# Ternary layers in five groups instead of six, with seeded banks for the last two, another order of slots and state-space layer, and one branch

## What is computed

```
x = x + 0.5 * _L0_ffn_ref(_layernorm(x), W1, W2, W3)            # gated layer, hidden 2048
x = x + _L0_attn_ref(_layernorm(x), qkv, o_proj, gamma, beta)
x = x + 0.5 * _L0_ffn_ref(_layernorm(x), W1, W2, W3)
x = x + 0.5 * _L1_ffn_ref(_layernorm(x), gate_w, up_w, down_w, gate_s, up_s, down_s)
x = x + _L1_attn_ref(_layernorm(x), B, C, D)                    # state-space layer
x = x + 0.5 * _L1_ffn_ref(_layernorm(x), gate_w, up_w, down_w, gate_s, up_s, down_s)

def _L1_ffn_ref(x, ...):     # ternary layer, weights in {-1, 0, 1}, hidden 1408 = 11 blocks of 128
    g = einsum('th,ih->ti', x, gate_w) * gate_s
    u = einsum('th,ih->ti', x, up_w) * up_s
    return einsum('ti,hi->th', silu(g) * u, down_w) * down_s

def _L1_attn_ref(x, B, C, D):
    return einsum('bsn,dn->bsd', tanh(einsum('bsd,nd->bsn', x, B)), C) + D * x
```

## Time and profile before

| | |
|---|---|
| median of 3 runs | 1855.29 us (1854.92 to 1859.22) |
| the profiled execution | 1855.78 us, its span 1853.9 us |
| PE matmul busy, share of the span | 1743.8 us, 94% |
| VectorE (DVE) | 1199.1 us, 65% |
| ScalarE (ACT) | 824.2 us, 44% |
| GpSimd | 121.4 us, 7% |
| matmuls in the program | 7696 |

### The profile page before, as it was taken

How to read it: one execution, slowest core, us unless ns; L and a number is a source line. 1 busy time by engine, 2 the same in 40 slices (tenths; PEclk the granted TensorE clock), 3 DMA queues, 4 the chain that set the end, 5 groups by cost and what they waited for, 6 DMA issues and landing times.

```text
span 1853.9 us, 21200 instructions
## 1 busy us (share of the span) xinstructions
PE 1743.8 (94%) x7696; PEld 1407.2 (76%) x7696; DVE 1199.1 (65%) x1843; ACT 824.2 (44%) x1347; POOL 121.4 (7%) x184
## 2 busy tenths in 40 slices
PE   6899999999978999899999999999989987899998
PEld 5688887788867888688888888887767766677676
DVE  8777678577754555554447444467688676767866
ACT  4544544465654343333223343234554545454443
POOL 1000000000021210000000000000000505000000
PEclk9899999999999999999999999999999999899999
DMA  8675553799944000154444444444555541256464
GB/s 309 228 267 205 204 204 141 310 363 366 373 171 173 21 1 1 56 199 153 154 153 154 153 153 154 153 183 174 205 204 210 199 171 52 102 205 237 172 222 187
DMA packets 61403, 340.34 MB, mean 184 GB/s; under 512 B 6256, under 2 KB 14832, under 8 KB 43760
## 3 DMA queue, kind: packets, MB, share of 16 engines
q1 hardware_dynamic: 52848, 334.73, 47.9%
q10 hardware_dynamic: 8448, 4.20, 0.8%
HBM read 259.73 MB, written 79.17 MB: 183 GB/s over the span
## 4 chain that ended last, share of the span: by engine, by line
PE 45%; DVE 8%; ACT 2%; issue 2%; POOL 0%; DVEq 0%; ACTq 0%; POOLq 0%
PE psum L420 18%; PE psum L422 14%; PE psum L424 12%; DVE xc_lo L1561 1%; PE psum L614 1%; DVE sg L1631 1%; DVE stats L1487 1%; DVE y L1593 1%; DVE y L1596 1%; DVE x L1605 1%; ACT psum L1084 1%; ACT xc_hi L992 0%; DVE y L1599 0%; DVE sg L1624 0%; DVE x L1591 0%
## 5 line engine op out<-in xcount | busy, mean ns | idle before, releaser
L420 PE MATMUL psum<-xc_hi,w 128*128 128x512 f32 x1544 | 621.1, 402 | 48.9 <-ACT psum L1166 18.4
L422 PE MATMUL psum<-xc_lo,w 128*128 128x512 f32 x1544 | 609.1, 394 | 0.0
L420 PEld LDWEIGHTS psum<-xc_hi,w 128*128 128x128 f32 x1544 | 294.0, 190 | 142.6 <-ACT psum L1084 32.2
L420 PE MATMUL psum<-w,hid 128*128 128x512 f32 x896 | 357.5, 399 | 28.8 <-ACT xs L974 8.8
L424 PE MATMUL psum<-xc_hi,w 128*128 128x512 f32 x928 | 365.7, 394 | 0.0
L424 PE MATMUL psum<-w,hid 128*128 128x512 f32 x896 | 352.6, 394 | 0.0
L422 PEld LDWEIGHTS psum<-xc_lo,w 128*128 128x128 f32 x1544 | 294.5, 191 | 57.9
L1591 DVE TENSOR_TENSOR x<-psum,x 128x512 f32<-128x512 f32 x256 | 172.9, 687 | 151.9 <-PE psum L424 151.9
L420 PEld LDWEIGHTS psum<-w,hid 128*128 128x128 f32 x896 | 170.4, 190 | 80.5 <-ACT psum L1191 14.9
L1613 DVE TENSOR_TENSOR hid<-sg,hid 128x512 fp32r<-128x512 f32 x224 | 159.7, 713 | 99.6 <-ACT hid L1099 80.7
L422 PE MATMUL psum<-w,hid 128*128 128x512 f32 x544 | 213.5, 392 | 0.0
(11 more groups left out here) (151 smaller groups left out, 1992.5 us busy)
## 6 DMA issues: line engine op xcount, KB each, us to landing
w<-w_kept SPq DMA_DIRECT2D x93, 1792.0 KB, 7.3
w<-w_kept SPq DMA_DIRECT2D x94, 512.0 KB, 8.2
w_kept<-w SPq DMA_DIRECT2D x16, 1792.0 KB, 7.6
w_kept<-prep SPq DMA_DIRECT2D x12, 1792.0 KB, 7.5
w_kept<-w SPq DMA_DIRECT2D x16, 512.0 KB, 6.8
w_kept<-prep SPq DMA_DIRECT2D x12, 512.0 KB, 8.6
x<-in_w2a SPq DMA_DIRECT2D x8, 512.0 KB, 8.1
att_raw<-in_att_w SPq DMA_DIRECT2D x4, 1024.0 KB, 7.7
```

Source lines behind the costliest of these rows:

```text
L420: pe.matmul(out, a_hi, b_hi, start=start, stop=False, skip_group_check=onto)
L422: last = pe.matmul(out, a_hi, b_lo, start=False, stop=stop and zero == "a", skip_group_check=onto)
```

## The change

- Ternary groups are now `(0,1,2)`, `(3,4)`, `(5,6)`, `(7,8)`, `(9,10)`. The third block of the first group is kept in two parts of `xs` (`hid_more`).
- The down tiles of slots 1 and 2 are gone; the first group stands in slots 3 and 4 with 6 matmuls a tile.
- Of the group `(7,8)`, tiles 0 to 3 are made and added in slot 9 as before. Tiles 4 to 7 are made in a new step `fill`, after p4 of slot 10, in the banks in which the last group then goes on accumulating. The last group's eight tiles have a bank each: 0, 4, 1, 3, 2 for tiles 0 to 4 (`END_BANKS`) and the ring's for 5 to 7. All eight are seeded with `y`; tiles 5, 6, 7 already in slot 9.
- ACT does `seed_y` ahead of both `hid_high` of the block before, and in some slots (`open`: 1, 2, 10) one of these later still. DVE's work for the layer norm and the sums is spread by tables (`LATE`, `FINISH`, `STATS`, `SUMS`), also over the first slots of the next pass, which add the last tiles and take the last conversions. New waits (`ended_before`) keep the next pass off banks 0 to 4 until their tile is read.
- State-space layer: `STATE_ORDER`, the orders of DVE and ACT, and the place of one `chunk` of GpSimd.
- PE has one branch around passes 4 to 7 and the state-space layer, instead of two with the state-space layer between them.

```diff
-          "B": [(0,)] + [(2 * g - 1, 2 * g) for g in range(1, HB // P // 2 + 1)],
+          "B": [(0, 1, 2)] + [(2 * g + 1, 2 * g + 2) for g in range(1, HB // P // 2)],
...
+END_BANKS = (BX, BV, BY, BW, BZ)
+SEED_ORDER = (5, 6, 7, 0, 1, 4, 2, 3)
+FILL_ORDER = (5, 6, 7, 4)
...
+SUMS = {4: {7: (0,), 8: (1,), 9: (2, 3)}, 5: {}, 6: {8: (0, 1), 9: (2, 3)}, 7: {}}
...
-               ("down", 1, range(TT)), ("up", 2, ()), ("up", 3, ()), ("next", 0, range(TT)), ("down", 2, range(2)),
-               ("next", 1, range(TT)), ("down", 2, range(2, TT)), ("down", 3, range(TT))]
+               ("down", 1, range(TT)), ("up", 2, ()), ("next", 0, range(TT)), ("up", 3, ()), ("next", 1, range(TT)),
+               ("down", 2, range(TT)), ("down", 3, range(TT))]
...
+            def fill(ps, exact):
+
+                g = len(ps.groups) - 2
+                group_wait(ps, g, 1)
+                for i in FILL_ORDER:
+                    pe.wait_ge(seeded, seeds_before(ps) + SEED_ORDER.index(i) + 1)
+                    last = group(ps, g, i, plan.bank["d", ps.downs[-1][i][2]], False, False, exact)
+                last.then_inc(fill_done, 1)
...
             with pe.If(flag == 0):
-                run(passes[4], True)
-                run(passes[5], True)
+                ternary(True)
             with pe.Else():
-                run(passes[4])
-                run(passes[5])
-            state_space()
-            with pe.If(flag == 0):
-                run(passes[6], True)
-                run(passes[7], True)
...
+            def ternary_end(ps):
+                u = ps.u0 + ps.n - 1
+                seed(ps, 0)
+                seed(ps, 1)
+                seed(ps, 4)
+                hid_high(u, 0)
+                convert_next(ps, 1)
+                seed(ps, 2)
+                act.wait_ge(fill_done, ps.no - BEFORE_B + 1)
+                hid_high(u, 1)
+                seed(ps, 3)
+                for m in range(2, 7):
+                    convert_next(ps, m)
...
             def state_space():
-                before = passes[BEFORE_S - 1]
-                finish(before, 0)
-                state_stats(2)
+                following = passes[BEFORE_S]
+                finish(passes[BEFORE_S - 1], 1)
                 state_low(0, 0)
-                finish(before, 1)
                 state_low(0, 1)
                 state_stats(3)
-                state_x_low(2, 0)
-                state_x_low(2, 1)
+                for i in range(TT):
+                    state_x_low(2, i)
...
+                state_stats(0)
+                for i in range(TT):
+                    state_x_low(3, i)
```

More of the change, by code:

```diff
@@ L99, in add_pass @@
             for g, i in tiles[s]:
-                self.down(ps.downs[s], g, i, 3)
+                self.before[self.d] = newest.get(i)
+                newest[i] = self.d
+                if s == ps.n and kind == "B" and i < len(END_BANKS):
+                    self.bank["d", self.d] = END_BANKS[i]
+                    self.user[END_BANKS[i]] = ("d", self.d)
+                    ps.downs[s].append((g, i, self.d))
+                    self.d += 1
+                else:
+                    self.down(ps.downs[s], g, i, 3)
                 if i == PT - 1:
@@ L1374, in _ @@
                 for s in range(ps.n):
-                    slot(ps, s)
-                tail(ps)
+                    if ps.kind == "A":
+                        up_slot(ps, s)
+                    else:
+                        ternary_slot(ps, s)
+                if ps.kind == "A":
+                    tail(ps)
+                else:
+                    ternary_end(ps)
         @block.gpsimd
@@ L1464, in _ @@
                 skip(s_tile(3, i), x[:, PT + TT + i, :])
+                if i == 1:
+                    chunk()
             chunk()
@@ L1667, in slot @@
                     w13_split(s + 1)
-                if ps.no in (5, 7) and s < 2:
-                    finish(passes[ps.no - 1], s)
                 if last:
@@ new lines, in ternary_end @@
+            def ternary_end(ps):
+                tiles, m = ps.downs[-1], 2
+                for k, tile in enumerate(tiles):
+                    if follower(ps) and k == len(END_BANKS):
+                        break
+                    add_tile(ps, *tile)
+                    if follower(ps) and k in (1, 3, 4):
+                        convert_next(ps, m)
+                        m += 1
+                    if ps.no == BEFORE_S - 1:
+                        if k == 1:
+                            convert_next(ps, 2)
+                        if k == TT - 1:
+                            finish(ps, 0)
+                            convert_next(ps, 3)
+                            state_stats(2)
```

371 lines of the change are left out of this document (257 added, 114 removed).

## The result

The changed kernel takes 1803.78 us (median of 4 runs, 1802.03 to 1807.32) against 1855.95 for the kernel before in 4 runs beside it: a ratio of 0.9718 with a 95% interval of 0.9699 to 0.9738. The forecast was 1809.2 us with a range of 1800 to 1828. The profiled execution took 1803.14 us with a span of 1801.3.

What follows compares the result with a forecast made beforehand. PE has the most work everywhere; only its 88.6 us of waits or slow running can change. Tails, branch, slots, state-space layer and pass 6 sum to -46.1: 1855.8 becomes 1809.7, as median 1809.2 us, range 1800 to 1828.

Steps and rivals of the forecast that it cites:

- The tails: After p4 of slot 10: no PE waits left; passes 4 and 6 -5.6 and -5.5 us, pass 7 -3.7.
- The branch: Before the state-space layer: jump moved behind the last matmul saves 3.6 us; tail of pass 5 -6.8 with it.
- DVE's work at nothing: Twelve adds fewer in each pass, 29 us of DVE, costed at nothing because matmuls cover them.
- The slots: Slots of passes 4, 5 and 7: -1.5, -5.7 and -0.1 us, with slot 2's weights 0.7 late.
- rival A: Weights bind the short slots, landing after 8.2 us: 22 us back, 1831 in all; chance 0.12.
- The small waits: PE's remaining waits in the slots, left at 0.4 us a slot, 4.4 a pass.
- The state-space layer: Its new order leaves waits of 4.1 us instead of 15.6: window 56.4 us, -9.4.
- down(2) stands behind `next` 0, whose banks ACT empties only after a normalisation that waits for GpSimd, and two tanhs: In the state-space layer: explains PE's one large wait, 8.75 us.
- Rival B: State-space layer keeps its length as a chain through DVE, GpSimd, ACT and PE: +13 us, 1822; chance 0.14.
- Pass 6: Its slots: `seed_y` 2.6 us late behind ACT's conversions, 2.0 of lowered clock; 113.2 us, -7.8.
- rival C: Short waits in slots 0 to 2 lower PE's clock to 1.2 GHz: +67 us, 1876; chance 0.04.
- Rival D: Waits only move, since DVE's adds weren't in the way: no change, 1855 us; chance 0.03.

Runs made afterwards that it cites:

- e4: Changed kernel with the last block's high part ahead of seeds 0, 1 and 4 in ACT's list: 1807.02 us, ratio 0.9737.
- e1: Changed kernel with the two branches of the kernel before: 1805.01 us, ratio 0.9719.
- h1: Changed kernel with two branches, and PE's last tile of pass 5 waiting until the tile before is finished: 1809.64 us in one run.
- e2: Kernel before with one branch around passes 4 to 7, nothing else changed: 1851.2 us, ratio 0.9972.
- e5: Changed kernel with twelve more unused DVE statistics instructions in each of passes 4 to 7, 30 us in all: 1806.06 us, ratio 0.9728.
- e3: Changed kernel with the old order of PE's list, ACT's copies and DVE's last adds in the state-space layer: 1806.27 us, ratio 0.9739.
- h5: Kernel before with DVE's statistics of half 1 moved ahead of chunk 2's first low part: 1846.80 us, ratio 0.9957.
- h6: e3 with DVE's statistics of half 1 put back behind chunk 2's first low part: 1809.22 us in one run.
- h2: Changed kernel with its one branch, and PE's last tile of pass 5 waiting until the tile before is finished: 1802.70 us.
- g1: Changed kernel with each slot's 1792 KB weight load issued as three transfers on two semaphores: 1799.92 us, ratio 0.9690.

## Why the prediction was right, and where it was not

**The tails: right.** The hand schedule said that no wait is left, and none is: 10.9 us each, which is 48 matmuls at 0.227 us. The 11.5 had 0.3 of reserve that wasn't needed and one step too many. e4 confirms the step that it named, the seeds' place, at 1 us. At the end the last finish came 15.0 us after the start of p4's last matmul, as forecast (18.8 less 15.0 is 3.8, where the prediction wrote 3.7); from there to the end of the span 3.1 us passed instead of 4.2, and that 1.1 is the part the prediction held to be unchanged (in the other kernels with the new end, the window varies from 17.3 to 18.4 us).

**The branch: the size of the window right by luck, the reason wrong.** The step that failed is that the change puts the jump behind the last matmul and so saves 3.6 us. In the changed kernel the place of the jump doesn't matter (e1, no gap). The gap is gone with the new tail, with one branch or two; it comes back when a wait holds PE's program just ahead of the jump (h1). In the kernel before, one branch instead of two gives 5.3 us in the median (e2): in the profiled execution 3.8 in its own window, taken back by 3.4 in the next, and 2.8 in pass 6 and the end, where the clock differs (the 1.48 us wait of pass 6 was followed by lowered clock in the kernel before and not in e2). The other 2.1 lie outside these windows and are not explained.

**DVE's work at nothing: right** to about 2 us for 30 us of work (e5). The share it was argued from is misread: DVE is busy 73 to 90 us in the slot windows of the earlier trace rows, not 73 to 85.

**The slots: mechanism right, two sizes off.** Slot 2 starts when its weights land; they take 8.2 us, not the 7.3 taken, with 512 KB issued right behind them. That was rival A's number, and A was real but small: six waits with 4.2 us in all, where A had up to 22. A needs 1.5 us in each of three slots of each pass; the longest is 1.4 and most slots have none. Slots 1 and 2 take 14.8, 14.5 and 15.1 us in passes 5 to 7 (14.5 forecast), 16.6 in pass 4 with the wait of 1.15 us for `seed_w` behind the normalisations, forecast at 1.3. The small waits were taken as 4.4 us a pass. Pass 4's window less its matmuls (102.6), the weights' 1.6 and the 1.3 leaves 4.6; but for pass 5, with 1.3 for the weights, 3.7 are left, and for pass 7, with 1.6, 2.1: 0.7 and 2.3 us too many.

**The state-space layer: number right, in part by luck, attribution incomplete.** 57.1 against 56.4. The waits forecast at down(0) and down(1), 1.4 and 2.5 us, are there at 1514.31 and 1525.11 with steps that are 0.86 and 2.88 too long, and the clock behind the second costs 1.5 where 1.0 was forecast; in other executions it cost nothing or 2.9. But the step "down(2) stands behind `next` 0, whose banks ACT empties only after a normalisation that waits for GpSimd, and two tanhs", with "In the new order up(3) and `next` 1 stand between" as its cure, named the last link and left out one that was late: the statistics of half 1 on DVE, behind a low part that waits for ACT. e3 restores what the step named, and the wait stays away; h5 and h6 move the statistics, and it goes by 4.7 and comes with 3.0. What stands behind the other 4.0 stays open. Rival B (the chain keeps the layer's length) is out for the changed kernel.

**Pass 6** starts with the forecast wait for `seed_y` (2.44 us for 2.6), and the clock behind it costs 1.7, forecast 2.0 (nothing in h1 and h2, with the same wait); most of the 1.6 us that it did better are again small waits.

**The clock, rival C: not seen.** The slot windows of passes 4, 5 and 7 ran at 1.00, with eleven waits of 0.2 to 1.4 us in them. What the Trainium skill, TensorE: Matmul & The Clock Gate, A second HAM failure mode, describes, a clock that swings because PE idles shortly between groups of matmuls, did not happen in these three windows. Rival D is out by the result.

## What to carry to other kernels

A wait's last releaser need not be what to mend: follow the chain back until an instruction stands ready behind one that is not, as the statistics did behind a low part, and exchange those two. A gap at a branch can go with the wait ahead of it, without touching the branch. Before a difference between two windows is put down to an edit, compare the granted clock behind the waits that both have: here it made up to 2.4 us in a window where nothing was changed. And work taken off an engine with slack (30 us here) is worth little by itself; the gain lies where PE no longer waits.

## What the runs showed of the hardware

- A jump over the other branch left a gap of 3.0 us on PE with a wait 4 matmuls ahead of it (h1) and of 3.6 in the kernel before, whose last tile got its seed 0.3 us before it started; with 16 matmuls behind the last wait there was none (e1).
- The same idle gap was paid for by the clock to a different amount from one execution to the next. Behind 2.84 us in the state-space layer the lowered clock cost nothing in e3, g1 and h6, 1.5 us in the changed kernel and 2.9 in h2; behind 2.44 at the start of pass 6 1.7 in the changed kernel and nothing in h1 and h2; behind 3.02 in h1 2.8.
- 1792 KB issued with 512 KB behind them landed after 8.2 us at the start of a pass; as three parts the first 1024 KB took 5.5 to 6.2, and once, issued at the same distance, 8.3.
